# Moving the normalisation for the second expert routing from VectorE to GpSimd in a 16-tile attention stage, and placing and scattering rows earlier

## What is computed

```python
x = x + _L0_attn_ref(_layernorm(x), ...)          # softmax over the 16 heads, 1/(1+dots) per head and channel
x = x + 0.5 * _L0_ffn_ref(_layernorm(x), ...)     # second use of the 4 experts
# in _L0_ffn_ref:
gate_logits = jnp.einsum('bld,de->ble', x, Wg) + bg
idx = jnp.argmax(jax.nn.softmax(gate_logits, axis=-1), axis=-1)
```

## Time and profile before

| stretch of the span | us | what runs |
|---|---|---|
| 0 to 283 | 283 | first routing and first 4-expert feed-forward |
| 283 to 510 | 227 | first attention with the second routing in it; the last scatter is issued by 510.4 |
| 510 to 528 | 18 | barrier, plan of the blocks, first loads |
| 528 to 2491 | 1963 | the other four layers |

### The profile page before, as it was taken

One profiled execution on the slowest core, in us unless ns is written; L12 is line 12 of the kernel. 1 busy time (PEld: TensorE's weight loads), 2 busy tenths in 40 slices (PEclk: granted clock), 3 DMA queues, 4 the chain that ended last, 5 costly groups with the idle time before them and its releaser, 6 DMA issues.

```text
span 2491.5 us, 36261 instructions
## 1 busy us (share of the span) xinstructions
PE 2240.4 (90%) x11234; PEld 1557.4 (63%) x11234; DVE 1979.6 (79%) x4646; ACT 1298.6 (52%) x1907; POOL 1010.9 (41%) x921
## 2 busy tenths in 40 slices
PE   4489488859679999997999999999999999999999
PEld 3367366637557777774555555555555556878787
DVE  6578488848568888877888888888888886888887
ACT  1088333248534444443666666666666665444444
POOL 5746535526545556553221111211112112565654
PEclk9999666679879999997999999999999999999999
DMA  7244212034277888861222111111111214888887
GB/s 178 71 153 137 39 32 42 26 127 148 71 153 167 183 170 183 179 137 56 69 69 64 59 61 59 56 61 59 56 59 57 67 45 102 182 177 186 177 186 154
DMA packets 141300, 265.27 MB, mean 106 GB/s; under 512 B 19999, under 2 KB 23082, under 8 KB 140918
## 3 DMA queue, kind: packets, MB, share of 16 engines
q1 hardware_dynamic: 129910, 242.61, 40.8%
q0 software_dynamic: 11264, 21.07, 3.3%
HBM read 212.92 MB, written 54.65 MB: 107 GB/s over the span
## 4 chain that ended last, share of the span: by engine, by line
PE 41%; DVE 5%; DMA 5%; issue 3%; ACT 1%; SPq 0%; POOL 0%; DVEq 0%; POOLq 0%; ACTq 0%
PE ps L2012 12%; PE ps L2036 10%; PE ps L2023 9%; DMA gate_rows<-gates_dram 4%; PE ps L1731 2%; DVE m L1415 2%; PE ps L1733 2%; PE ps L1732 2%; PE ps L2045 1%; PE ps L2078 1%; DMA gates_dram<-gateT 1%; DVE shift L1578 1%; DVE lo L1089 1%; PE ps L1745 1%; PE ps L2070 1%
## 5 line engine op out<-in xcount | busy, mean ns | idle before, releaser
L1578 DVE TENSOR_REDUCE shift<-ps 128x1 fp32r<-128x512 f32 x1024 | 663.9, 685 | 146.8 <-PE ps L2012 142.1
L1012 ACT ACTIVATE prob<-ps 128x1024 f32<-128x1024 f32 x512 | 510.0, 1025 | 354.1 <-PE ps L2023 346.6
L861 ACT ACTIVATE hi<-m 128x512 fp32r<-128x512 f32 x512 | 318.9, 631 | 415.2 <-DVE m L1415 415.2
L711 POOL TENSOR_TENSOR lo<-m,hi 128x512 fp32r<-128x512 f32 x256 | 349.9, 1371 | 373.1 <-ACT hi L861 373.0
L2012 PE MATMUL ps<-k_pad,q_st 128*128 128x512 f32 x1024 | 401.0, 433 | 14.5 <-DVE shift L1578 7.6
L1415 DVE SCALAR_TENSOR_TENSOR m<-ps,gate_rows 128x512 f32<-128x512 f32 x512 | 334.4, 680 | 80.4 <-PE ps L1733 50.5
L2012 PEld LDWEIGHTS ps<-k_pad,q_st 128*128 128x128 f32 x1024 | 179.4, 190 | 257.1 <-DVE shift L1578 176.1
L2023 PE MATMUL ps<-q_sh,k_pad 128*128 128x512 f32 x1024 | 330.0, 404 | 0.0
L2036 PE MATMUL ps<-prob,v_cols 128*32 128x512 f32 x2048 | 272.7, 605 | 0.4 <-ACT prob L1012 0.4
L1089 DVE TENSOR_TENSOR lo<-m,hi 128x512 fp32r<-128x512 f32 x256 | 220.7, 862 | 17.1
L1731 PE MATMUL ps<-hi,vals_hl 128*128 128x512 f32 x512 | 210.1, 410 | 2.9 <-DVE lo L1089 2.6
(11 more groups left out here) (215 smaller groups left out, 3923.9 us busy)
## 6 DMA issues: line engine op xcount, KB each, us to landing
gate_rows<-gates_dram SPq DMA_DIRECT2D x256, 512.0 KB, 11.9
w_blk<-w_dram SPq DMA_DIRECT2D x38, 514.5 KB
q_st<-q_dram SPq DMA_DIRECT2D x64, 256.0 KB, 2.6
k_pad<-k_dram SPq DMA_DIRECT2D x256, 50.0 KB
k_dram<-qk_hl SPq DMA_DIRECT2D x48, 256.0 KB
q_dram<-qk_hl SPq DMA_DIRECT2D x48, 256.0 KB
x_blk<-sorted_x SPq DMA_DIRECT2D x38, 258.0 KB
x<-y_dram POOLq DMA_DIRECT2D x16, 256.0 KB
```

Source lines behind the costliest of these rows:

```text
L711: pool.tensor_tensor(m["lo"][:, s], m["m32"][:, s], m["hi"][:, s].bitcast(F32), ALU.subtract).then_inc(sig(ph, "lo_pool"), 1)
L861: return act.activation(o, i, ACT.Copy)
L1012: act.activation(prob[:, h % HP, 2 * half:2 * half + 2, :], ps[:, b0:b0 + 2, :], ACT.Exp, scale=SCALE).then_inc(sig(ph, "prob"), 1)
L1578: dve.tensor_reduce(shift[:, g % 2, b, c:c + 1], wide(PASS1 + b % 2), AXX, ALU.max, negate=True).then_inc(sig(ph, "qmax"), 1)
```

## The change

The normalisation for the second routing leaves VectorE. GpSimd does it in step t for tile t-1 (before: VectorE, step t, tile t-2), in three instructions: copy of the token numbers, subtraction of the mean, product with the reciprocal root, with one wait between the last two. VectorE gets one new wait, before `moments(2, t-1)`, for GpSimd's normalisation of tile t-3, since that reads the same copy of `mv2`. `place(t-3)` moves on VectorE from behind `minus_attn` to right behind `plus_eps`. GpSimd's scatter of a tile comes in the same step as its place, behind root, collect and the new normalisation, so GpSimd's order becomes root, collect, normalise t-1, scatter t-3, and it has one step less.

```diff
+            def apply_norm0(t):
+                dst, mean, rs = xnr[2][t % XR], mv2[(t + 1) % 2][:, 1, :, 0:1], rs2[(t + 1) % 2][:, 1]
+                if t >= XR:
+                    pool.wait_ge(moved[t // 4 % MOVES], 512 + 256 * (t // XR))
+                pool.tensor_copy(dst[:, :, D], token[:, t * BLK:t * BLK + BLK])
+                every = [P, BLK, D]
+                pool.tensor_tensor(dst[:, :, 0:D], x[:, t * BLK:t * BLK + BLK, :], mean.broadcast_to(every),
+                                   ALU.subtract).then_inc(sig(2, "centred"), 1)
+                pool.wait_ge(sig(2, "centred"), t + 1)
+                pool.wait_ge(sig(1, "rstd"), t + 6)
+                pool.tensor_tensor(dst[:, :, 0:D], dst[:, :, 0:D], rs.unsqueeze(2).broadcast_to(every),
+                                   ALU.mult).then_inc(sig(2, "xn"), 1)
...
-            for t in range(-6, TILES + 4):
+            for t in range(-6, TILES + 3):
                 def here(n):
                     return 0 <= t + n < TILES
-                if here(-4):
-                    scatter(2, t - 4)
                 if here(6) and t < 1:
                     collect(t + 6)
                 if both(t):
                     root(1, t + 5, t % 2, both(t))
                 if here(6) and t >= 1:
                     collect(t + 6)
+                if here(-1):
+                    apply_norm0(t - 1)
+                if here(-3):
+                    scatter(2, t - 3)
...
-                    if here(-2):
-                        apply_norm(2, t - 2, (t - 1) % 2, 1, t + 4)
...
                     if here(-1):
                         add_y(t - 1)
+                        if t >= 3:
+                            dve.wait_ge(sig(2, "xn"), TILES + t - 2)
                         moments(2, t - 1, mv2[t % 2][:, 1])
...
                         plus_eps(1, t % 2, both(t))
+                    if here(-3):
+                        place(2, t - 3)
...
                         minus_attn(t, t % 4)
-                    if here(-3):
-                        place(2, t - 3)
```

## The result

The changed kernel takes 2509.3 us (median of six runs, 2508.05 to 2512.16); the kernel before, run in turn with it, 2496.23 us (six runs, 2493.25 to 2500.53). The ratio is 1.0052, with a 95% interval of 1.0041 to 1.0063: slower by some 13 us.

A forecast was written before the change was run, and what follows sets the result against it. VectorE was taken as the bound at 12.11 us a step, with an equally long ring through TensorE and ScalarE. Terms -1.3 + 1.0 + 1.0 + 3.9 = +4.6 us gave 2504 us, range 2490 to 2513.

The forecast's parts named there:

- The likeliest case: Steady step of 11.8 to 12.1 us with the stage's longer end paid: +4.6 us in sum; chance 0.62.
- rival 2: `prod` or `outT` waits behind GpSimd's subtraction in every step, 0.80 us instead of 0.15: +13 us, 2513; chance 0.24.
- t = 1, 2 (steps 1 to 2, 2 to 3): First two routing steps: 0.5 us each for VectorE and GpSimd meeting at SBUF, +1.0 us.
- nine steady steps (3 to 12): Each step falls from 12.11 to 11.97 us, a gain of 0.14; -1.3 us together.
- last steps (12 to 16): Work taken from VectorE gives nothing there; `place` gains 0.29, the meeting at SBUF costs 0.5: +0.2 a step, +1.0 us.
- tail: End of the stage: normalisations of the last tiles delay GpSimd's last scatter by 3.9 us, bounds 2.5 and 4.5.
- Both engines at SBUF: VectorE's two-SBUF-input instructions wait for GpSimd's subtraction or product: 0.15 us a steady step, bounds 0 and 0.80.
- the ring through TensorE and ScalarE: From `outT` over TensorE's list, ScalarE's copy and exponential back to `outT`: 12.11 us, 11.82 once `place` moves.
- rival 3: Something other than GpSimd's last scatter releases the barrier, so the stage's end costs nothing: +0.7 us, 2501; chance 0.03.
- rival 1: VectorE is the bound and regains 1.14 us a step, TensorE perhaps granted 2.4 GHz more often: -12 us, 2488; chance 0.15.
- the other way to be wrong: GpSimd takes 1.3 us or more for each of its two operations; its step of 12 us becomes the bound.
- The wait ahead of `ssum`: VectorE idle for the exponential: 0.8 to 1 us a step instead of 0.32, named as a sign in the profile after.

The follow-up runs named there:

- e5: The kernel before with only `place` and the scatter moved, the normalisation staying on VectorE; 2495.85 us, ratio 0.9994.
- e7: The changed kernel with ScalarE's exponential put ahead of its copy of `rows_in`, nothing else; 2508.14 us, ratio 1.0042.
- e9: The changed kernel with GpSimd's normalisation put between the second and third scatter of its step; 2516.48 us, ratio 1.0082.
- e1: The changed kernel with GpSimd's normalisation put ahead of the collect DMA instead of behind it; 2496.17 us, ratio 1.0029.
- e4: The changed kernel without GpSimd's subtraction and product (zeros routed), and with ScalarE's exponential ahead of its copy of `rows_in`; 2473.79 us, one run.
- e3: The changed kernel without GpSimd's subtraction and product, so zeros are routed and the output is not the reference's; 2480.38 us, one run.
- e8: The kernel before with `place` and scatter moved, ScalarE's exponential ahead of its `rows_in` copy, and the second routing's normalisation on ScalarE; 2485.01 us, ratio 0.9951.
- e2: The changed kernel with GpSimd's normalisation put behind the four scatters of its step; 2499.74 us, ratio 1.0040.
- e6: The kernel before with `place` and scatter moved and ScalarE's exponential ahead of its copy of `rows_in`; 2495.35 us, ratio 0.9992.

## Where the prediction held and where it failed, point by point

The likeliest case did not come. I had put 0.62 on a difference within 0.3%, with 4.6 us more as the sum; it became 13.1 us more (0.5%). The time, 2509.3, lies inside the range, but with some luck. The range was laid out from 2500.04, the median of three runs of the kernel before; with three more it is 2496.23. As a difference the range ends at +13, and +13.1 stands at that very edge. This is rival 2, whose price was +13, at a chance of 0.24.

| term | predicted, us | measured, us |
|---|---|---|
| t = 1, 2 (steps 1 to 2, 2 to 3) | +1.0 | +1.8 |
| nine steady steps (3 to 12) | -1.3 | +9.8 |
| last steps (12 to 16) | +1.0 | +0.2 |
| tail | +3.9 | +3.0 |
| sum | +4.6 | +14.8 in the profiled stage, +13.1 by medians |

*The step that failed is "Both engines at SBUF": 0.15 us a step.* Measured in the step shown: `pi` +1.25 (1.47 against 0.22) and `prod` +0.69, so VectorE is held for 1.9 us (1.4 to 2.0 over the steps from t = 3 to 9), and the step grew by 1.3. Two errors lie in it. First, the placing. I had the subtraction start 3.3 us behind root's start, with `prod` past. It starts 392.40 - 389.90 = 2.50 behind, since root took 1.68 us and not 2.02 (the move of `place` and scatter alone does that, 1.67 in e5) and the collect and the copy together some 0.8 and not 1.3. And `pi`, which started 1.7 us behind root before (383.03 against 381.34, from `prod` in the earlier trace rows less 0.20 and 0.22), now starts 2.46 behind: `place` stands ahead of it now, 0.29, and the longer wait for the exponential, 0.48. Thus `pi` meets the whole subtraction and `prod` most of the product. I had moved `place` and laid out GpSimd's list without moving `pi` by it. The shift of `pi` by itself matters little: in e7 `pi` comes half a microsecond earlier, is held all the same, and the step is the same. Second, the bound. I took the row's loss of 0.80 as the most that one step can lose. That row was one VectorE instruction that began with one GpSimd instruction; here two instructions of VectorE meet two of GpSimd, and a small one loses as much as a large one (e9: 2.1 us on two instructions of 0.17). The upper bound should have been all of GpSimd's normalisation, 2.6 us by its rows (392.24 to 394.85); e7 lost 2.4.

*The mechanism of rival 2 was right, its place was not.* I had put the held instruction on the ring through TensorE and ScalarE and priced it at 0.80 - 0.29. That ring has no part in it (e7). The chain is `plus_eps` on VectorE, root, collect, copy, subtraction and product on GpSimd, `prod` on VectorE, and then VectorE's list round to `plus_eps`. By the rows of the steady step: 389.64 to the product's end at 394.85 is 5.21; `prod` ends 0.56 later; VectorE's list from there to 403.09 takes 7.68. Together 13.45. In all seven steps from t = 3 to 9 `prod` ends 5.67 to 5.77 us behind `plus_eps`, and the list takes 7.68 to 7.70. That it is a chain and not an account that merely adds up is what e1 tests: collect taken out of it, 13.45 - 0.96 = 12.49, measured 12.49. So rival 2's total, +13, was near for partly wrong reasons: it had +0.5 for each of the nine steady steps, which on average lost 1.1 (9.8 / 9), and made up for that with +2.5 in the last steps, which lost 0.2, and +4.5 in the tail, which lost 3.0.

*What was right.* VectorE's list without the normalisation was put at 10.97: e4 shows 11.02. That a ring close behind would eat much of the gain was right in kind and too high in size: 11.82 laid out, 11.41 on average in e3. With it, the norm off VectorE at no other cost would have been worth 0.7 us a step, not 0.29. The new wait of VectorE for GpSimd's tile shows nowhere. GpSimd kept up. The tail was to be +3.9 with bounds of 2.5 and 4.5 and was +3.0: the normalisation of tile 15 added 2.3 us and not 2.5, and GpSimd began the last root 0.75 us later behind `plus_eps` than before, and not 1.2. Here the working also has a slip: 1.2 + 2.5 + 5.2 is 8.9 and not 9.1, so its own terms give +3.7. The end of the last scatter does set the end of the stage (`table` follows 6.63 us behind it, before and after), so rival 3 is out. Where the prediction says that the rule on the ports gives "the last rival below", it is rival 2 that is meant. Root holds nothing in the steady steps: `x_low` takes 0.68 right beside it. The granted clock did not move, 0.61, so rival 1's way to a shorter ring was not taken. GpSimd's operations take 1.04 us when alone, so the other way to be wrong, 1.3 us for each, did not come either; the subtraction's row of 1.34 is one that overlaps the copy's.

*The tests named in the prediction* pointed the right way: "over 12.3 for rival 2" was measured at 13.45. The wait ahead of `ssum`, 0.8 to 1 us if I was right, is 0.78 to 1.13, and yet I was not. It says that the exponential is late at that point, and not what sets the step: e7 takes the wait away, and the step stays. It should not have been a sign.

*Open.* From which moment VectorE is held: `pi` in e7 and `equal` in e9 stand still 0.4 to 0.5 us before the row of GpSimd's copy begins, and GpSimd's spans are rough. The collect and the scatter that run just then are not it: in e8 `pi` starts in the middle of a collect and takes 0.22, and in the changed kernel `equal` takes 0.18 beside a scatter. Why root holds neither `pi` nor `x_low`, though it reads and writes SBUF as well. Why the stage of e2 is 15.1 us longer but its time only 10.5; part of it is that the code behind its stage took 1977.5 us, the least of all, where the kernel before took 1981.1.

## What to carry to other kernels

Work moved from VectorE to GpSimd is not off VectorE if both have it at SBUF in the same microseconds: 1.14 us taken from VectorE's list brought 1.4 to 2.0 us of standing still. Bound the loss by all that GpSimd runs beside VectorE's instructions on SBUF, however small these are, and look first whether ScalarE has the room: the same work there brought VectorE no standing still, and the time fell by 0.5% (e8), where all the rest of that edit gave nothing that can be measured (e6). Where an edit is laid out on two engines' lists, shift both lists by every part of it before asking what meets what, and ask too whether the held engine feeds the one that holds it; then a loop is closed, and every instruction in front of the holding one (here a collect of 0.96 us) is on it.

## What the runs showed of the hardware that I had not expected

- A VectorE instruction of 0.17 us took 1.77 us beside GpSimd's copy and subtraction (e9), one of 0.22 us 1.95 (e7): two of GpSimd's instructions in a row pass ahead of one that waits.
- VectorE's `xn`, a tensor with scalars per partition, is held like the two-input ones: four of them took 3.52 us instead of 1.11 (e2). `stats`, with one SBUF input, is not: it took 0.87 us, started beside GpSimd's product (365.42 and 365.44 in e2).
- GpSimd's power (root, 1.68 us) held neither `x_low` (0.68, started 0.11 us behind it) nor, before, `pi` (224 to 226 ns in all sixteen). The Trainium skill ("SBUF — State Buffer", section "SBUF: two separate sides") makes no such exception for a GpSimd instruction that reads SBUF; here the rows decide.
- Root of 128x8 took 1.68 us in the changed kernel and 2.04 before. The moved `place` and scatter alone bring it to 1.67 (e5, from t = 3 on); why, no run tells.
